# One SBUF tile of 128 bytes for five small code tiles, and the norm weights allocated ahead of the output weights

## The chip, the core and the metric

The program runs on one core of one Trainium2 chip. The metric is device time in microseconds, the median over several executions. The kernel before has a median of 848.24 us over 3 runs (843.49 to 848.28).

## The reference, cut to what matters

Four layers work on `x` of shape (2, 256, 512) with a context of (2, 512, 512), each on a normalised `x` and with a residual. Layer 0 is an attention with quantised inputs followed by a linear layer whose 4-bit weights come from a look-up table. Layer 1 is a latent attention of 16 heads and a gated feed-forward layer of inner width 1376 with ternary weights. Layer 2 is the large one, an attention of 32 query heads of 128 in 8 groups of key and value heads:

```python
q = rmsnorm(x @ q_proj.T) * q_norm_w      # 32 heads of 128
k = rmsnorm(ctx @ k_proj.T) * k_norm_w    # 8 heads of 128
v = ctx @ v_proj.T                        # 8 heads of 128
x = x + softmax(q @ k.T * 128 ** -0.5 + mask) @ v @ o_proj.T
```

It is followed by a routing step that selects tokens, a small convolutional gate, and a linear layer with eight low-rank experts (the tail).

## The kernel before, in words

The kernel is written engine by engine. Each layer is a function with one block; in a block every engine has its own list of instructions, and semaphores join them. All loads go through the queue of SyncE. The order on each engine is written out by hand, and nothing in it depends on the address of a tile.

**Tiles and their addresses.** `Core.sbuf` (line 87) takes a tile from a stack: the tile begins where the one before it ended, rounded up to a multiple of 32 bytes within the partition. A tile that lives as long as the kernel is taken from the outer stack, one of a layer from the layer's own, which is given back at its end. So every tile behind a changed one moves with it. `Codes.__init__` (line 111) takes five tiles of 128 x 4 float32, 16 bytes in each partition, that is 5 x 32 = 160 bytes of addresses. They hold scales of the feed-forward layer of layer 1 (lines 122 to 160, 1435 and 1464). Behind them come the small tiles of the ternary weights and then all tiles of all layers. Only `context_parts` (line 941) is taken from the other end of the memory and has an address of its own.

**Layer 2.** `layer2_attention` (line 1650) runs 16 steps, one per group of heads and batch. TensorE makes every float32 product from two rounded parts of each operand, in three matmuls of type float32r: `product` (line 1867, the matmul is line 1873). In each matmul 128 columns of a stationary tile are loaded as weights, and a moving tile of 256 or 512 columns is streamed past them. The products and their tiles, moving tile first, are: keys and values from `wkv2` and `context_parts` (256 columns, 48 matmuls a step), queries from `wq2` and `xnT2` (512 columns), scores from `keysT2` and `queriesT2` (512), the mix of values from `probsT2` and `values2` (256 columns, 48 matmuls a step), and the output from `wo2` and `headsT` (512). Between them stand transposes of 128 x 128 (lines 1929 and 1950). ScalarE, VectorE and GpSimd empty the banks and make the parts; VectorE also counts for the selection of tokens that the tail needs (line 2487). `norm_weights` (line 1677) is a tile of 8 bytes, loaded by two small transfers at the start of layer 2 (line 1746) and read by the scaling of the keys.

**Other places.** The tail makes its last products in the same way, from `wb` and `xnT_parts` (line 2720) and from `bm_parts` and `lowT` (line 2744). Layer 1 makes its latent queries from `latentT` and `wqk` (line 1076).

Of the kernel before, what the change touches and what calls it, by code (L numbers as in the profile page):

```python
# [13 lines left out]
F32, BF16, I32, U16, F32R = mybir.dt.float32, mybir.dt.bfloat16, mybir.dt.int32, mybir.dt.uint16, mybir.dt.float32r  # L14
# [4 lines left out]
P = 128  # L19
B, SEQ, D = 2, 256, 512  # L20
CTX = 512
TILES = B * SEQ // P
# [10 lines left out]
class Own:  # L33


    def __init__(self, engine, semaphore):
        self.engine, self.semaphore, self.count = engine, semaphore, 0
# [71 lines left out]
class Codes:  # L109

    def __init__(self, k):
        small = lambda name: k.sbuf("codes_" + name, [P, TILES], F32)
        self.beta, self.betae, self.binv, self.gate_scale, self.up_scale = (
            small(x) for x in ("beta", "betae", "binv", "gate_scale", "up_scale"))
        self.beta_ready, self.codes_ready, self.turned_psum, self.turned_ready, self.gate_psum, self.up_psum, \
            self.scales_ready = (k.keep("codes_" + x) for x in (
                "beta_ready", "codes_ready", "turned_psum", "turned_ready", "gate_psum", "up_psum", "scales_ready"))
# [1521 lines left out]
def layer2_attention(k, dram):  # L1639
# [17 lines left out]
    with ExitStack() as s:  # L1657
        ctxT2, wq, wkv = gw.ctxT2, gw.wq, gw.wkv
        xnT2 = k.sbuf("xnT2", [P, 2, KT, TILES * P], F32R, s)
        wo = k.sbuf("wo2", [P, 2, REP, D], F32R, s)  # L1660
        raw_o = gw.raw_q
        rows = k.xn
# [11 lines left out]
        keysT = k.sbuf("keysT2", [P, 2, B * CTX], F32R, s)  # L1674
        values = k.sbuf("values2", [P, 2, CTILES, HD], F32R, s)
        mask = k.sbuf("mask", [P, TPB, CTX], F32, s)
        weights = k.sbuf("norm_weights", [P, 2], F32, s)
        keyscale = weights
        probs = k.sbuf("probs2", [P, 3, CTX], F32, s)
        probsT = k.sbuf("probsT2", [P, 2, 2, CPB, SEQ], F32R, s)  # L1680
# [1294 lines left out]
def build(nc, dram, out):  # L2975
    ternary = nc.dram_tensor("ternary", (INNER, D), BF16, kind="Internal").ap()
    inverse = nc.dram_tensor("inverse_sums", (P, 8), F32, kind="Internal").ap()
    with ExitStack() as stack:
        k = Core(nc, stack)
        k.inverse_dram = inverse  # L2980

        def run(*layers):
            for layer in layers:
                k.begin(layer)
                layer(k, dram)

        with ExitStack() as context:
            with ExitStack() as first:
                k.ternary = TernaryWeights(k, first, dram, ternary)
                k.latent = LatentWeights(k, first)  # L2990
                run(layer0)
                k.context = ContextParts(k, context)
                run(layer1_attention)
            with ExitStack() as third:
                k.group_weights = GroupWeights(k, third, dram)
                run(layer1_ffn, layer2_attention)
        k.out = out
        run(tail)
# [62 lines left out]
```

How the kernel before makes its waits and increments, by code:

```python
    def wait(self):  # L43
        self.engine.wait_ge(self.semaphore, self.count)
# [79 lines left out]
def codes_magnitude_scalar(k, n, t, absolute):  # L124
    k.nc.scalar.wait_ge(k.tile_xn, TILES * n + t + 1)
    if t:
        k.nc.scalar.wait_ge(k.codes.beta_ready, t)
    k.nc.scalar.activation(absolute, k.xn[:, t, :], ACT.Abs, accum_out=k.codes.beta[:, t:t + 1])\
     .then_inc(k.codes.beta_ready, 1)
# [2 lines left out]
def codes_inverse_vector(k, h):  # L132
    v, own, q, half = k.nc.vector, k.vown, k.codes, half_of(h)
    v.wait_ge(q.beta_ready, TPB * (h + 1))
    own(v.tensor_scalar(q.beta[:, half], q.beta[:, half], 1.0 / D, None, ALU.mult))
    own.wait()
    own(v.tensor_scalar(q.betae[:, half], q.beta[:, half], EPS, None, ALU.add))
    own.wait()
    own(v.reciprocal(q.binv[:, half], q.betae[:, half]))
    own.wait()
# [29 lines left out]
def codes_turn_tensor(k, t, codes, bank):  # L170
    pe = k.nc.tensor
    pe.wait_ge(k.codes.codes_ready, t + 1)
    for f in range(KT):
        last = pe.transpose(bank.bitcast(BF16)[:, f * P:(f + 1) * P], codes[:, f * P:(f + 1) * P], k.ident16[:, :])
    last.then_inc(k.codes.turned_psum, 1)
# [2 lines left out]
def codes_turned_scalar(k, t, bank):  # L178
    a = k.nc.scalar
    a.wait_ge(k.codes.turned_psum, t + 1)
    a.copy(k.gate_up.turned[t], bank.bitcast(BF16).rearrange("p (f c) -> p f c", f=KT)).then_inc(k.codes.turned_ready, 1)
# [42 lines left out]
    def wait(self):  # L224
        value = self.base + self.count
        self.engine.wait_ge(self.semaphore, value if self.i is None else self.i * self.per + value)
```

## Time and profile before

| what | value |
|---|---|
| median of 3 runs | 848.24 us (843.49 to 848.28) |
| the profiled execution: its time, and its span | 848.75 us, 846.6 us |
| mean granted TensorE clock, as a share of full speed | 0.979 |
| TensorE matmul busy | 776.7 us |
| VectorE busy | 692.8 us |
| ScalarE busy | 517.6 us |
| GpSimd busy | 431.9 us |
| bytes moved by DMA | 60.51 MB, 71 GB/s over the span |

Layer 0 lasts to about 65 us, the attention of layer 1 to 190, its feed-forward layer to about 231, layer 2 to 772, and the tail to the end. The time of an execution is 2.15 us longer than its span. Matmuls are pipelined and their ends are modelled, so a matmul's own duration is longer than its distance to the next one. Where a row of the timeline joins x matmuls, its length is (x - 1) distances and one duration; the distance from one start to the next is called the pitch below.

### The profile page before, as it was taken

The numbers are of one execution on the slowest core, as the hardware profiler recorded it, in microseconds if no ns is written. First come the engines' busy times: TensorE is split into PE (matmuls) and PEld (weight loads), VectorE is DVE, ScalarE is ACT, GpSimd is POOL, SyncE is SP. The second block draws the span as 40 slices with busy tenths as digits, with TensorE's granted clock in tenths as the row PEclk, the third lists the DMA queues.
The fourth block names the chain that finished last, engine by engine and source line by source line (L and its number), as shares of the span: only waits on it lengthen the run. The fifth ranks groups of instructions, "written<-read, shape, count | busy, mean of one in ns | idle before, by whom it ended". The sixth has DMA issues, their size and how long they took to land. (4 is left out here: it accounts for less than half of the span.)

```text
span 846.6 us, 16363 instructions
## 1 busy us (share of the span) xinstructions
PE 776.7 (92%) x5140; PEld 633.9 (75%) x5140; DVE 692.8 (82%) x1767; ACT 517.6 (61%) x1399; POOL 431.9 (51%) x388
## 2 busy tenths in 40 slices
PE   1987799978988999999999999999999999978888
PEld 0485566644677898898888989989889889866347
DVE  7878898989987887887887887788878878876986
ACT  6865789856466657657657657665675675641421
POOL 3136058924236745754745746745754764665110
PEclk9998999989999999999999999999999999999999
DMA  8245145403111220320320320320310210003001
GB/s 312 98 128 185 49 137 173 136 23 120 32 70 25 77 76 3 97 75 0 99 75 0 99 75 0 99 71 4 99 50 25 75 50 25 26 1 111 11 0 50
DMA packets 33452, 60.51 MB, mean 71 GB/s; under 512 B 5313, under 2 KB 14593, under 8 KB 33282
## 3 DMA queue, kind: packets, MB, share of 16 engines
q1 hardware_dynamic: 33410, 59.99, 21.7%
q8 instruction: 21, 0.34, 0.2%
q14 instruction: 21, 0.17, 0.1%
HBM read 57.47 MB, written 2.52 MB: 71 GB/s over the span
## 5 line engine op out<-in xcount | busy, mean ns | idle before, releaser
L2487 DVE TENSOR_SCALAR_CACHE_REDUCE xn<-ctxT,candidate 128x512 bf16<-128x512 f32 x240 | 168.8, 741 | 0.0
L2134 ACT ACTIVATE layer_attention_probs<-xnT,stats 128x512 f32<-128x512 f32 x128 | 94.1, 735 | 113.1 <-DVE stats L2269 113.1
L2281 DVE TENSOR_TENSOR layer_attention_probsT<-bank,layer_attention_probsT 128x512 fp32r<-128x512 f32 x128 | 88.1, 688 | 52.8 <-ACT layer_attention_probsT L2142 51.5
L1873 PE MATMUL bank<-layer_attention_keysT,layer_attention_queriesT 128*128 128x512 f32 x384 | 120.0, 420 | 4.6 <-DVE layer_attention_queriesT L2262 4.6
L1873 PEld LDWEIGHTS bank<-layer_attention_probsT,layer_attention_values 128*128 128x128 f32 x768 | 98.8, 189 | 13.0 <-DVE layer_attention_probsT L2281 3.7
L2142 ACT CAST layer_attention_probsT<-bank 128x512 fp32r<-128x512 f32 x128 | 75.0, 586 | 54.7 <-PE bank L1950 54.5
L1873 PE MATMUL bank<-layer_attention_probsT,layer_attention_values 128*128 128x256 f32 x768 | 102.3, 282 | 4.0 <-DVE layer_attention_xnT L2327 2.1
L1873 PE MATMUL bank<-layer_attention_l_wq,layer_attention_xnT 128*128 128x512 f32 x408 | 99.3, 392 | 0.0
L1873 PE MATMUL bank<-layer_attention_l_wkv,layer_context_parts 128*128 128x256 f32 x720 | 93.5, 282 | 0.0
L1873 PEld LDWEIGHTS bank<-layer_attention_l_wkv,layer_context_parts 128*128 128x128 f32 x720 | 91.1, 188 | 2.5
L1873 PE MATMUL bank<-layer_attention_wo,layer_attention_headsT 128*128 128x512 f32 x336 | 88.7, 405 | 0.0
L2269 DVE CUSTOM_DVE_ANT_0 xnT<-bank,layer_attention_mask 128x512 f32<-128x512 f32 x128 | 87.1, 680 | 0.6 <-PE bank L1873 0.5
L1873 PEld LDWEIGHTS bank<-layer_attention_l_wq,layer_attention_xnT 128*128 128x128 f32 x408 | 75.3, 188 | 15.8 <-issue 0.2
L1816 POOL TENSOR_TENSOR layer_attention_mixed<-layer_attention_mixed,xnT 128x512 f32<-128x512 f32 x30 | 48.8, 1626 | 71.3 <-DMA xnT<-inverse_sums 43.8
L1950 PE MATMUL bank<-ident,layer_attention_probs 128*128 128x128 f32 x512 | 77.3, 274 | 3.1 <-ACT layer_attention_probs L2134 3.1
L1950 PEld LDWEIGHTS bank<-ident,layer_attention_probs 128*128 128x128 f32 x512 | 62.2, 141 | 14.2 <-issue 4.1
L1873 PEld LDWEIGHTS bank<-layer_attention_keysT,layer_attention_queriesT 128*128 128x128 f32 x384 | 62.6, 190 | 10.9 <-issue 5.5
L1873 PEld LDWEIGHTS bank<-layer_attention_wo,layer_attention_headsT 128*128 128x128 f32 x336 | 59.9, 188 | 11.5
L1801 POOL TENSOR_SCALAR layer_attention_ssq<-layer_attention_ssq 128x4 f32<-128x4 f32 x48 | 9.8, 205 | 89.0 <-ACT layer_attention_squares L2093 89.0
L2093 ACT ACTIVATE layer_attention_squares<-bank 128x128 f32<-128x128 f32 x192 | 52.0, 297 | 0.0
L1316 ACT ACTIVATE layer_attention_probs<-bank,layer_attention_negmax 128x512 f32<-128x512 f32 x64 | 44.8, 705 | 11.8 <-DVE layer_attention_negmax L1202 11.5
L1803 POOL TENSOR_TENSOR layer_attention_ssq<-layer_attention_ssq,minus_half 128x4 f32<-128x4 f32 x48 | 48.8, 1017 | 4.0
(352 smaller groups left out, 1648.5 us busy)
## 6 DMA issues: line engine op xcount, KB each, us to landing
layer_attention_l_raw_qo<-in_wqT SPq DMA_DIRECT2D x8, 1024.0 KB, 5.5
layer_attention_l_raw_qo<-in_woT SPq DMA_DIRECT2D x8, 1024.0 KB, 6.5
xnT<-inverse_sums SPq DMA_DIRECT2D x15, 512.0 KB, 3.7
tw_raw<-in_w_gateT SPq DMA_DIRECT2D x8, 688.0 KB, 4.0
tw_raw<-in_w_upT SPq DMA_DIRECT2D x8, 688.0 KB, 4.0
tw_raw<-in_w_downT SPq DMA_DIRECT2D x6, 768.0 KB, 5.0
layer_attention_l_raw_kv<-in_wkvT SPq DMA_DIRECT2D x8, 512.0 KB, 5.2
layer_ctx<-in_ctx SPq DMA_DIRECT2D x2, 1024.0 KB, 8.9
```

What stands on the lines that cost most here:

```text
L1316: a.activation(probs[:, u % 4, :], S[u % 3][:, :], ACT.Exp, bias=negmax[:, tile(u), head(u):head(u) + 1], accum_out=sums[:, tile(u), head( ...
L1801: own(g.tensor_scalar(ssq[:, c, :], ssq[:, c, :], 1.0 / HD, EPS, ALU.mult, ALU.add))
L1803: own(g.tensor_tensor(ssq[:, c, :], ssq[:, c, :], k.minus_half[:, 0:REP], ALU.pow))
L1816: g.tensor_tensor(now, now, factors, ALU.mult).then_inc(S_["mix_scaled"], 1)
L1873: last = pe.matmul(out, stationary[f][a], moving[f][b], start=f == 0 and x == 0, stop=f == count - 1 and x == 2)
L1950: last = pe.transpose(T[u % 2][:, c * P:(c + 1) * P], probs[:, u % 3, c * P:(c + 1) * P], k.ident[:, :])
L2093: return a.activation(squares[:, h, :], source, ACT.Square, accum_out=ssq[:, c, h:h + 1])
L2134: a.activation(probs[:, u % 3, :], masked[:, u % 2, :], ACT.Exp, bias=negmax[:, u:u + 1], scale=-1.0, accum_out=sums[:, u:u + 1]).then_inc ...
L2142: a.copy(probsT[:, 0, p % 2, :, u % 2 * P:(u % 2 + 1) * P], T[u % 2][:, :].rearrange("p (c q) -> p c q", c=CPB)).then_inc(S_["probsT_high" ...
L2269: v.tensor_tensor_reduce(masked[:, u % 2, :], S[u % 2][:, :], mask[:, u % TPB, :], -1.0, 3.4e38, ALU.add, ALU.min, negmax[:, u:u + 1]).the ...
L2281: v.tensor_tensor(probsT[:, 1, p % 2, :, columns], T[u % 2][:, :].rearrange("p (c q) -> p c q", c=CPB), probsT[:, 0, p % 2, :, columns], A ...
L2487: own(k.nc.vector.tensor_scalar((k.flags if flags is None else flags)[:, r % 2], row_tile(k.ctxT, r), k.candidate[:, r:r + 1].bitcast(F32) ...
```

## The change: what it does

The five code tiles become the first five rows of one tile of 128 x 8 x 4 float32, which takes 128 bytes. `norm_weights` is taken right behind `xnT2` instead of behind `mask`. No instruction is added, removed or moved on any queue.

```diff
 class Codes:
     def __init__(self, k):
-        small = lambda name: k.sbuf("codes_" + name, [P, TILES], F32)
-        self.beta, self.betae, self.binv, self.gate_scale, self.up_scale = (
-            small(x) for x in ("beta", "betae", "binv", "gate_scale", "up_scale"))
+        small = k.sbuf("codes", [P, 8, TILES], F32)
+        self.beta, self.betae, self.binv, self.gate_scale, self.up_scale = (small[:, x, :] for x in range(5))
...
         xnT2 = k.sbuf("xnT2", [P, 2, KT, TILES * P], F32R, s)
+        weights = k.sbuf("norm_weights", [P, 2], F32, s)
         wo = k.sbuf("wo2", [P, 2, REP, D], F32R, s)
...
         mask = k.sbuf("mask", [P, TPB, CTX], F32, s)
-        weights = k.sbuf("norm_weights", [P, 2], F32, s)
         keyscale = weights
```

All tiles behind the code tiles begin 32 bytes lower, since 128 bytes stand where 160 stood. In layer 2 the 32 bytes of `norm_weights` make up for it from `wo2` to `mask`, which keep their addresses; behind `mask` the tiles are again 32 bytes lower. The first byte of the tiles that matter, within the partition, and its remainder by 64:

| tile | before | after |
|---|---|---|
| `context_parts` (stationary for keys and values) | 196576 (32) | the same |
| `wkv2` (moving for keys and values) | 76096 (0) | 76064 (32) |
| `xnT2`, `wq2` | 96576 (0), 59712 (0) | 96544 (32), 59680 (32) |
| `raw_kv`, `raw_qo` (landing places of weights) | 84288 (0), 88384 (0) | 84256 (32), 88352 (32) |
| `wo2`, `headsT` | 112960 (0), 139648 (0) | the same |
| `keysT2`, `queriesT2` | 151936 (0), 131456 (0) | the same |
| `values2` (stationary for the mix) | 160128 (0) | the same |
| `probs2`, `probsT2` (moving for the mix) | 172448 (32), 178592 (32) | 172416 (0), 178560 (0) |
| layer 0: `bits`, `tree`, `weightT` | 149536, 166048, 215200 (32) | 32 lower (0) |
| layer 1 attention: `latentT`, `wqk`, all others | 131392, 90432 (0) | 32 lower (32) |
| tail: `raw_wb`, `wb`, `xnT_parts`, `lowT`, `bm_parts` | 105632, 113824, 136480, 157856, 161952 (32) | 32 lower (0) |

## Rows read from the trace of the kernel before

**Rows 1.** The page, busy time of each engine.
```profile
PE 776.7 (92%) x5140; PEld 633.9 (75%) x5140; DVE 692.8 (82%) x1767; ACT 517.6 (61%) x1399; POOL 431.9 (51%) x388
```

**Rows 2.** Windows by stage; columns as in the first line.
```profile
core 0: us, PE busy (x) PEld busy (x) DVE busy (x) ACT busy (x) POOL busy (x), PEclk, DMA share, GB/s
0.00:65.00 65.00, 43.24 (x243) 29.65 (x244) 51.05 (x101) 46.22 (x71) 18.14 (x26) 0.95 0.52 182
...
300.00:730.00 430.00, 429.35 (x2762) 382.84 (x2760) 348.56 (x967) 271.45 (x818) 250.40 (x219) 1.00 0.17 53
...
772.00:846.00 74.00, 64.05 (x330) 41.24 (x328) 56.32 (x178) 22.06 (x60) 9.48 (x15) 0.95 0.16 49
```

**Rows 3.** Waits of TensorE, 231 to 772 us: total, times, longest; the longest row.
```profile
PE bank L1873 <- DVE layer_attention_queriesT L2262: 4.6, 4, 2.0
```

**Rows 4.** Instruction groups, shapes apart: float32r products, count, busy us, mean ns.
```profile
L1873 PE MATMUL bank<-layer_attention_probsT,layer_attention_values 128*128 128x256 f32 x768 | 102.3, 282 | 4.0 <-DVE layer_attention_xnT L2327 2.1 <-DVE layer_attention_probsT L2281 1.2
...
L1873 PE MATMUL bank<-layer_attention_l_wq,layer_attention_xnT 128*128 128x512 f32 x408 | 99.3, 392 | 0.0
...
L1873 PE MATMUL bank<-layer_attention_l_wkv,layer_context_parts 128*128 128x256 f32 x720 | 93.5, 282 | 0.0
...
L1634 PE MATMUL bank<-layer_attention_l_wkv,layer_context_parts 128*128 128x256 f32 x48 | 6.8, 291 | 0.0
```

**Rows 5.** Timeline of TensorE in layer 2: start us, length us, what, xcount.
```profile
451.24 2.70 PE L1873 MATMUL bank<-layer_attention_l_wq,layer_attention_xnT 128*128 128x512 f32 x11
...
454.00 0.60 PE L1950 MATMUL bank<-ident,layer_attention_probs 128*128 128x128 f32 x4
...
466.41 1.45 PE L1873 MATMUL bank<-layer_attention_probsT,layer_attention_values 128*128 128x256 f32 x11
...
468.96 2.26 PE L1873 MATMUL bank<-layer_attention_wo,layer_attention_headsT 128*128 128x512 f32 x9
...
476.55 2.92 PE L1873 MATMUL bank<-layer_attention_l_wkv,layer_context_parts 128*128 128x256 f32 x23
```

**Rows 6.** Timeline of TensorE in layer 1 and in the tail, same columns.
```profile
81.51 0.64 PE L1076 MATMUL bank<-layer_attention_latentT,l_wqk 128*128 128x256 f32 x4
...
208.81 2.97 PE L190 MATMUL bank<-layer_attention_gate_up,layer_ffn_x4T 128*128 128x512 bf16 x13
...
832.06 5.30 PE L2720 MATMUL bank<-tail_wb,tail_xnT_parts 128*128 128x512 f32 x22
...
840.42 2.47 PE L2744 MATMUL bank<-tail_bm_parts,tail_lowT 128*128 128x512 f32 x10
```

**Rows 7.** Instruction groups, shapes apart: other engines at either address class.
```profile
L2281 DVE TENSOR_TENSOR layer_attention_probsT<-bank,layer_attention_probsT 128x512 fp32r<-128x512 f32 x128 | 88.1, 688 | 52.8 <-ACT layer_attention_probsT L2142 51.5
...
L2142 ACT CAST layer_attention_probsT<-bank 128x512 fp32r<-128x512 f32 x128 | 75.0, 586 | 54.7 <-PE bank L1950 54.5
...
L2262 DVE TENSOR_TENSOR layer_attention_queriesT<-bank,layer_attention_queriesT 128x512 fp32r<-128x512 f32 x32 | 22.1, 692 | 27.1 <-ACT layer_attention_queriesT L2126 27.1
...
L2126 ACT CAST layer_attention_queriesT<-bank 128x512 fp32r<-128x512 f32 x32 | 19.2, 599 | 19.2 <-PE bank L1929 18.7
...
L1772 POOL TENSOR_TENSOR layer_attention_l_wkv<-layer_attention_l_raw_kv,layer_attention_l_wkv 128x1024 fp32r<-128x1024 f32 x7 | 16.9, 2410 | 5.3 <-ACT layer_attention_l_wkv L2152 5.3
...
L667 DVE COPY_PREDICATED layer_tree<-layer_bits,layer_tree 128x2048 f32<-128x2048 uint16 x4 | 9.9, 2484 | 0.0
...
L950 POOL TENSOR_TENSOR layer_context_parts<-ctxT,layer_context_parts 128x1024 fp32r<-128x1024 f32 x4 | 9.5, 2372 | 0.3
...
L667 DVE COPY_PREDICATED layer_tree<-layer_bits,layer_tree 128x1024 f32<-128x1024 uint16 x4 | 5.3, 1313 | 0.1
```

**Rows 8.** Weight loads: their issues (KB, us to landing) and a reader's idle time.
```profile
layer_attention_l_raw_qo<-in_woT SPq DMA_DIRECT2D x8, 1024.0 KB, 6.5
...
tail_raw_wb<-in_wbT SPq DMA_DIRECT2D x1, 1024.0 KB, 7.5
...
L2164 ACT CAST layer_attention_wo<-layer_attention_l_raw_qo 128x2048 fp32r<-128x2048 f32 x7 | 13.4, 1914 | 0.0
```

## The prediction, made before the changed kernel ran

> **What bounds the kernel now.** I began with the page's busy times: TensorE is busy for 776.7 us, 92% of the span [rows 1]. That is an average over stages, so I cut the span into windows by stage [rows 2]. The reader is to see two things there. From 300 to 730 us TensorE is busy for 429.35 of 430 us at a full clock of 1.00 (2.4 GHz), while VectorE has 348.56 us of work. In layer 0 and in the tail no engine is full. So layer 2 lasts as long as the matmuls take to pass through TensorE. The waits of TensorE agree: from 231 to 772 us its longest entry is 4.6 us, in four waits [rows 3]. Whatever changes the rate of the matmuls in layer 2 reaches the end of the kernel in full, and what changes another engine there by a few per cent does not.
>
> Then I read the timeline of TensorE for the pitch of each product, since the mean duration of a matmul says nothing on its rate: both products of 256 columns show 282 ns [rows 4]. A row of x matmuls gives (length - one duration) / (x - 1). With 0.39 us for a matmul of 512 columns and 0.28 us for one of 256:
> - queries (2.70 - 0.39) / 10 = 231 ns, output (2.26 - 0.39) / 8 = 234 ns, mix (1.45 - 0.28) / 10 = 117 ns, keys and values (2.92 - 0.28) / 22 = 120 ns [rows 5];
> - tail, `wb`: (5.30 - 0.39) / 21 = 234 ns; tail, `bm_parts`: (2.47 - 0.39) / 9 = 231 ns; layer 1, `latentT`: (0.64 - 0.28) / 3 = 120 ns; a bf16 product of 512 columns, with its duration of 0.38: (2.97 - 0.38) / 12 = 216 ns [rows 6].
>
> So a float32r matmul of 512 columns needs 15 to 18 ns more than one in bf16, and the amount is not the same for each pair of tiles. The pairs `wb` and `xnT_parts` in the tail and `wq2` and `xnT2` in layer 2 have the same shapes and the same three-part loop, and differ by 3 ns. What differs is the distance of their addresses: 36864 bytes (9 x 4096) for the 231 ns of the queries, 4096 for the 231 ns of `bm_parts`, and 26688 and 22656, no multiples of 4096, for the two at 234 ns. This is why I don't cost the change at nothing from the start: it moves tiles against each other.
>
> **The change part by part.** *Instructions, queues, waits.* None is added, removed or moved. The three transfers at the start of layer 2 (mask and two norm weights) keep their places on SyncE's queue, and GpSimd's list is the same. Cost 0, and this needs no cover.
>
> *The one code tile.* Its readers are scalar operands of the feed-forward layer and get another address. Cost 0.
>
> *Pairs whose distance stays.* `wq2` and `xnT2` move together; `wo2`, `headsT`, `keysT2`, `queriesT2` stay; `latentT` and `wqk`, `wb` and `xnT_parts`, `bm_parts` and `lowT` move together. What could change is their remainder by 64. The rows exclude a price for that: `wq2` and `xnT2` both begin at a multiple of 64 and `bm_parts` and `lowT` both 32 beyond one, and both pairs have 231 ns; `wo2` with `headsT` and `wb` with `xnT_parts` are such a couple at 234 ns [rows 5, 6]. Cost 0.
>
> *Pairs whose distance changes.* There are two. The mix goes from 18464 to 18432 bytes (`probsT2` to `values2`), and keys and values from 120480 to 120512 (`context_parts` to `wkv2`). The mix has 768 matmuls, keys and values 720 + 48 = 768 [rows 4]. No row has their new distances. The pitches seen at 256 columns are 117 and 120 ns [rows 5, 6], so within what was seen the mix can lose 3 ns and keys and values can win 3 ns: 768 x 3 = 2.3 us, up for the one and down for the other. The outer bounds are wider. Below is the pitch of transposes of 128 x 128 of the same type, (0.60 - 0.27) / 3 = about 109 ns [rows 5]: (117 - 109) x 768 + (120 - 109) x 768 = 6.1 + 8.4 = 14.5 us gained. Above, I let the same excess double: 14.5 us lost. I take 0 for the sum: the nearest rows are the two pairs' own pitches and that of `latentT` and `wqk`, which lie within 3 ns and don't say which way a pair goes. The ends for the range are -2.3 and +2.3 us from the nearest rows, and -14.5 and +14.5 from the far ones.
>
> The Trainium skill ("SBUF — State Buffer", section "Who interferes with whom") says that TensorE has two read ports, one for the moving operand and one for the weight load, which are independent, and that TensorE waits for no other engine. By that the distance of two tiles has no price, and this part is exactly 0; the 3 ns between two pairs of the same shapes are not explained by it, so I keep the bounds of the rows.
>
> *Writes and reads of the other engines at the other remainder.* `probsT2` begins 32 bytes beyond a multiple of 64, `queriesT2` at one: VectorE writes them in 688 and 692 ns, ScalarE in 586 and 599. GpSimd makes a part of `context_parts` (32) in 2372 ns and of `wkv2` (0) in 2410 [rows 7]. There is no gain in being at 0; the difference is 2% and the other way. In layer 2 this is hidden behind TensorE in any case; without that cover it would be 128 x 4 ns = 0.5 us on VectorE. Cost 0.
>
> *Layer 0, `tree`.* This is not covered. The choice between leaves takes (2484 - 1313) / 1024 = 1.14 ns per element at remainder 32 [rows 7], and no row has it at 0. At one element in 1.04 ns, the slope that 688 ns for 512 leaves if its fixed part is 155 ns (my estimate from that row), the groups shown would win 9% of 9.9 + 5.3 = 15.2 us, or 1.4 us. The other end is the same loss. By the rows on the remainder I take 0.
>
> *Loads.* Weights come to land at remainder 32. A load of 1 MB to remainder 0 took 6.5 us, one to remainder 32 took 7.5 us among others in the tail [rows 8]. At worst each load is 1.0 us later; ScalarE, which reads them, shows 0.0 us of idle time before those reads [rows 8], so they are early. Cost 0; if that slack were gone, what is late next is ScalarE's rounding and then GpSimd's, at 1.0 us per group.
>
> The sum is 0 against the profiled execution of 848.75 us, which lies 0.5 us above the median of 848.24. I keep the median as the base: **848 us**.
>
> **The rivals.** *Equal remainders pay (faster).* After the change the two tiles of every float32r pair have the same remainder by 64; before, the mix (32 and 0) and keys and values (0 and 32) did not. If that made the whole excess over 109 ns go, 14.5 us are won: about 834 us; half of it gives 841. For it: the two pairs are unequal now and lie 8 and 11 ns above the transposes. Against it: the pairs that are already equal still need 231 to 234 ns where bf16 needs 216, and `latentT` with `wqk`, equal too, needs 120 [rows 5, 6]. Chance of more than 1%: 0.11.
>
> *The two streams collide more (slower).* The mix comes to a distance of 9 x 2048 bytes. If the moving stream and the weight load then meet more often, the place is the 768 mixes, and with keys and values 1536 matmuls in a stage that TensorE fills. The nearest row is `latentT` with `wqk`, at 20 x 2048: 120 ns, so +2.3 us, 850.5 us. It decides from 5.5 ns on each of the 1536, 8.5 us; with the excess doubled it gives 863 us. Against it: no pair of 256 columns shows more than 120 ns. Chance of more than 1%: 0.07.
>
> *Only layers 0 and tail gain.* Then 1.4 us at most in layer 0, about 847. It lies within the forecast.
>
> *The change does nothing at all*, because no tile moves: excluded by the rounding to 32 bytes, 160 against 128, and it would give the same 848.
>
> **How the numbers follow.** Below 1%, about 8.5 us, a measurement of this kernel can't tell a difference from none; its runs span 843.49 to 848.28. The forecast (sum 0, within 2.3 us for each pair, 1.4 us in layer 0) has 0.82, all of it within 1%. The faster rival has 0.11, the slower 0.07. The range takes the run spread with the near bounds (843.5 - 2.3 - 1.4 = about 840 below) and half of the slower rival's far bound above (848.2 + 7.3 = about 855); beyond it lie the two rivals' far halves and less than 2 in 10.
>
> **What would show it.** In the timeline of layer 2 the mix should stay at 117 to 120 ns and keys and values too; queries at 231 and output at 234 must not move at all, or distance is not what matters. The window from 300 to 730 us should still show TensorE full. VectorE's 688 ns and ScalarE's 586 ns for `probsT2` should be the same within 2%, and the 2484 ns of the choice in layer 0 shows whether the remainder counts there. The prediction is wrong if the mix or keys and values come near 109 ns, or over 123.

## The result and the profile after

The changed kernel takes 849.88 us (median of 21 runs, 846.71 to 852.72), the kernel before 847.48 us over 21 runs beside it. The ratio is 1.0028, with an interval of 1.0016 to 1.0040: slower by 2.4 us, which these runs can tell from none. The time lies within 1% and inside the range. The forecast of no difference at all is refuted. The profiled execution took 849.88 us, its span is 847.7 us and its mean granted clock 0.976.

The page of the changed kernel, then its windows by stage, then the longest wait of TensorE in layer 2, against [rows 1 to 3]:

```profile
PE 777.4 (92%) x5134; PEld 634.9 (75%) x5140; DVE 692.1 (82%) x1767; ACT 516.9 (61%) x1399; POOL 432.0 (51%) x388
```
```profile
0.00:65.00 65.00, 42.73 (x247) 28.50 (x248) 53.66 (x110) 47.78 (x73) 19.29 (x28) 0.97 0.53 188
300.00:730.00 430.00, 429.30 (x2758) 382.60 (x2757) 347.84 (x966) 271.06 (x819) 250.74 (x219) 1.00 0.16 52
772.00:846.00 74.00, 65.11 (x328) 41.45 (x325) 55.75 (x177) 21.96 (x60) 9.46 (x15) 0.93 0.15 45
```
```profile
PE bank L1872 <- DVE layer_attention_queriesT L2261: 4.6, 4, 2.0
```

TensorE is as full as before. The row to read is the count: in the same 430 us it starts 2758 matmuls where [rows 2] had 2762. So each takes a little longer, and that shows in no busy time. A count depends on where the window cuts a step, though; the period of a step, below, is the better measure.

The timeline of TensorE in layer 2 of the changed kernel, against [rows 5]:

```profile
441.12 2.99 PE L1872 MATMUL bank<-layer_attention_l_wkv,layer_context_parts 128*128 128x256 f32 x24
...
452.96 2.92 PE L1872 MATMUL bank<-layer_attention_l_wq,layer_attention_xnT 128*128 128x512 f32 x12
...
464.25 1.60 PE L1872 MATMUL bank<-layer_attention_probsT,layer_attention_values 128*128 128x256 f32 x12
```

The mix now has (1.60 - 0.28) / 11 = 120 ns where it had 117. Keys and values have (2.99 - 0.28) / 23 = 118 ns where they had 120. Queries stay at (2.92 - 0.39) / 11 = 230 ns. Two pairs got another distance, and the pitches of those two moved, in opposite directions.

What the pitches come to is read from the period of a step. In each step SyncE issues one transfer of the sums of the softmax, so two such rows twelve steps apart give the mean step. The timeline of SyncE, first of the kernel before, then of the changed one:

```profile
303.07 0.34 SPq L1729 DMA_DIRECT2D inverse_sums<-stats  x1
...
699.73 0.34 SPq L1729 DMA_DIRECT2D inverse_sums<-stats  x1
```
```profile
300.71 0.34 SPq L1728 DMA_DIRECT2D inverse_sums<-stats  x1
...
697.91 0.34 SPq L1728 DMA_DIRECT2D inverse_sums<-stats  x1
```

Before: (699.73 - 303.07) / 12 = 33.055 us. After: (697.91 - 300.71) / 12 = 33.100 us. Over 16 steps that is +0.7 us. Two traces of kernels with the same distances in layer 2 agree within 0.012 us a step (the run "All layers but layer 2" below against before), so 0.045 is more than their spread. The trace splits it: I summed the distance from each matmul's start to the next one's over these twelve steps, product by product. A step's mix takes 5.791 us instead of 5.691 (16 x 0.100 = +1.6 us), keys and values 5.658 instead of 5.738 (-1.3 us), and all other matmuls together 0.025 us more (+0.4 us). So the two pairs make +0.3 of the +0.7 us.

The other engines did not change. Groups of instructions of the changed kernel, shapes apart, against [rows 7]:

```profile
L2280 DVE TENSOR_TENSOR layer_attention_probsT<-bank,layer_attention_probsT 128x512 fp32r<-128x512 f32 x128 | 88.1, 688 | 53.1 <-ACT layer_attention_probsT L2141 51.9
...
L2141 ACT CAST layer_attention_probsT<-bank 128x512 fp32r<-128x512 f32 x128 | 74.9, 585 | 55.7 <-PE bank L1949 55.7
...
L1771 POOL TENSOR_TENSOR layer_attention_l_wkv<-layer_attention_l_raw_kv,layer_attention_l_wkv 128x1024 fp32r<-128x1024 f32 x7 | 16.8, 2403 | 5.6 <-ACT layer_attention_l_wkv L2151 5.6
...
L666 DVE COPY_PREDICATED layer_tree<-layer_bits,layer_tree 128x2048 f32<-128x2048 uint16 x4 | 9.9, 2472 | 0.0
...
L666 DVE COPY_PREDICATED layer_tree<-layer_bits,layer_tree 128x1024 f32<-128x1024 uint16 x4 | 5.3, 1326 | 0.1
```

Each is within 1% of its row before, with its tile 32 bytes lower.

**The rest of the 2.4 us.** The two profiled executions differ by 1.1 us. Up to the first load of layer 2 the changed kernel is 2.4 us ahead, its steps lose 0.65 us, the end of layer 2 loses 1.2 us and the tail 1.7 us. The last two go with TensorE's granted clock, and the first at least in part (0.97 in layer 0 where [rows 2] had 0.95). Windows over the end of layer 2 and the first part of the tail, before and after:

```profile
732.56:771.80 39.24, 31.36 (x180) 25.49 (x178) 31.95 (x72) 13.53 (x33) 29.14 (x24) 1.00 0.04 14
771.80:825.03 53.23, 45.91 (x235) 26.12 (x235) 43.35 (x146) 17.65 (x52) 9.48 (x15) 0.94 0.17 49
```
```profile
730.80:771.21 40.41, 32.75 (x180) 27.10 (x178) 31.95 (x72) 13.52 (x33) 29.16 (x24) 0.96 0.05 14
758.40:761.80 3.40, 3.40 (x14) 3.01 (x13) 3.23 (x6) 0.96 (x2) 3.32 (x4) 0.50 0.00 0
771.21:826.10 54.89, 47.53 (x234) 26.59 (x235) 43.36 (x146) 17.56 (x52) 9.46 (x15) 0.91 0.16 47
```

The same 180 matmuls take 1.2 us longer, and the middle row shows why: from 758.4 to 761.8 us the clock is 0.50 (1.2 GHz). The timeline shows what TensorE did ahead of it, before and after:

```profile
758.99 1.67 PE L1873 MATMUL bank<-layer_attention_probsT,layer_attention_values 128*128 128x256 f32 x12 [2.12 <-DVE layer_attention_xnT L2327]
```
```profile
757.23 2.00 PE L1872 MATMUL bank<-layer_attention_probsT,layer_attention_values 128*128 128x256 f32 x12 [2.12 <-DVE layer_attention_xnT L2326]
```

It had waited for the same 2.12 us in both, and the clock fell in one of them. So a single profile says little outside the steps. Over the 216 runs of the whole kernel in these comparisons (each kernel with its own mean, one slope for all), 0.001 less of mean clock goes with 0.51 us more of the span (standard error 0.03). At a clock of 0.979 the kernel before stands at 845.8 us (87 runs) and the changed one at 847.25 (21 runs, standard error 0.27): +1.4 us.

### The profile page after: what moved, and what is told of

It is laid out like the page before. It is cut to its first block and busy times, and to the rows that moved or that the text cites. A ratio compares the mean times of both kernels' runs of the same rounds, so it can differ in the third digit from the quotient of the medians.

```text
span 847.7 us, 16357 instructions
## 1 busy us (share of the span) xinstructions
PE 777.4 (92%) x5134; PEld 634.9 (75%) x5140; DVE 692.1 (82%) x1767; ACT 516.9 (61%) x1399; POOL 432.0 (51%) x388
## 5 line engine op out<-in xcount | busy, mean ns | idle before, releaser
L2280 DVE TENSOR_TENSOR layer_attention_probsT<-bank,layer_attention_probsT 128x512 fp32r<-128x512 f32 x128 | 88.1, 688 | 53.1 <-ACT layer_attention_probsT L2141 51.9
L1872 PE MATMUL bank<-layer_attention_keysT,layer_attention_queriesT 128*128 128x512 f32 x384 | 120.1, 421 | 4.6 <-DVE layer_attention_queriesT L2261 4.6
L1872 PEld LDWEIGHTS bank<-layer_attention_probsT,layer_attention_values 128*128 128x128 f32 x768 | 100.6, 190 | 12.5 <-DVE layer_attention_probsT L2280 3.9
L2092 ACT ACTIVATE layer_attention_squares<-bank 128x128 f32<-128x128 f32 x192 | 51.9, 297 | 0.0
```

The costliest lines, as they stand in the source:

```text
L1872: last = pe.matmul(out, stationary[f][a], moving[f][b], start=f == 0 and x == 0, stop=f == count - 1 and x == 2)
L2092: return a.activation(squares[:, h, :], source, ACT.Square, accum_out=ssq[:, c, h:h + 1])
L2280: v.tensor_tensor(probsT[:, 1, p % 2, :, columns], T[u % 2][:, :].rearrange("p (c q) -> p c q", c=CPB), probsT[:, 0, p % 2, :, columns], A ...
```

## The experiments

Theory 1 says that the distance between the moving and the stationary tile sets the pitch of a float32r product, and that TensorE hands this on to the end. Its rivals change with the question; each expectation names them. The first three edits are shown against the changed kernel.

**Only the code tiles.** `norm_weights` goes back to its old place, so that keys and values alone get their new distance.

```diff
 xnT2 = k.sbuf("xnT2", ...)
-weights = k.sbuf("norm_weights", [P, 2], F32, s)
 wo = k.sbuf("wo2", ...)
...
 mask = k.sbuf("mask", ...)
+weights = k.sbuf("norm_weights", [P, 2], F32, s)
```

> The code tiles alone: all later tiles 32 bytes lower, norm weights left behind the mask. Keys and values get the new distance (120512), the mix keeps its old one (18464). Theory 1 (only the distance of the two tiles of a product counts): keys and values near 118 ns as in the changed kernel, the mix at 117 as before, so 768 x 2 = 1.5 us faster than before, ratio about 0.998; a step of layer 2 about 0.1 us shorter. Theory 2 (the 32 bytes cost something in the other layers, some 1.7 us): about the same as before, ratio 1.000. Theory 3 (addresses count for nothing, the change was chance): ratio 1.000 and both pitches as before.

Measured: 847.79 us, ratio 0.9998 (0.9980 to 1.0016). The time alone doesn't choose between the theories, whose ratios of 0.998 and 1.000 both lie in the interval; the pitches speak for theory 1. In the timeline keys and values have (1.58 - 0.28) / 11 = 118 ns, the mix (1.57 - 0.28) / 11 = 117 ns:

```profile
465.46 1.57 PE L1872 MATMUL bank<-layer_attention_probsT,layer_attention_values 128*128 128x256 f32 x12
...
471.25 1.58 PE L1872 MATMUL bank<-layer_attention_l_wkv,layer_context_parts 128*128 128x256 f32 x12
```

**Only the norm weights.** The five code tiles are five again, so that the mix alone gets its new distance.

```diff
-small = k.sbuf("codes", [P, 8, TILES], F32)
-self.beta, ... = (small[:, x, :] for x in range(5))
+small = lambda name: k.sbuf("codes_" + name, [P, TILES], F32)
+self.beta, ... = (small(x) for x in ("beta", ...))
```

> The norm weights alone: the code tiles as before, tiles from the output weights to the mask 32 bytes higher, all others as before. The mix gets the new distance (18432), keys and values keep the old one. Theory 1: the mix near 120 ns, keys and values at 120, so 768 x 3 = 2.3 us slower, ratio about 1.0027, a step of layer 2 about 0.14 us longer. Theory 2: the same 2.3 us, since no other layer moves. Theory 3: ratio 1.000.

Measured: 850.10 us, ratio 1.0027 (1.0009 to 1.0045). The mix has (1.60 - 0.28) / 11 = 120 ns:

```profile
465.72 1.60 PE L1873 MATMUL bank<-layer_attention_probsT,layer_attention_values 128*128 128x256 f32 x12
```

The SyncE rows of the two, codes first:

```profile
302.41 0.34 SPq L1728 DMA_DIRECT2D inverse_sums<-stats  x1
...
698.40 0.34 SPq L1728 DMA_DIRECT2D inverse_sums<-stats  x1
```
```profile
301.87 0.34 SPq L1729 DMA_DIRECT2D inverse_sums<-stats  x1
...
699.77 0.34 SPq L1729 DMA_DIRECT2D inverse_sums<-stats  x1
```

Their steps are 32.999 and 33.158 us, -0.056 and +0.103 against before. The sum, +0.047, is the changed kernel's +0.045. So the change is two changes of opposite sign, and the norm weights alone make it slower.

**All layers but layer 2.** The code tiles are merged, and layer 2 is put back by a pad of 32 bytes ahead of its first tile, with the norm weights behind `mask` again. The feed-forward layer of layer 1, whose tiles stand behind the pad, is put back with it. (`self.begin` is the address of a tile of that layer; it moves with the pad.)

```diff
-self.begin = base + 4 * KT * (2 * GW2 + ...)
+self.begin = base + 32 + 4 * KT * (2 * GW2 + ...)
...
+sb("pad", [P, 8], F32)
 self.wq = sb("wq2", [P, 2, KT, GW2], F32R)
...
 xnT2 = k.sbuf("xnT2", ...)
-weights = k.sbuf("norm_weights", [P, 2], F32, s)
...
 mask = k.sbuf("mask", ...)
+weights = k.sbuf("norm_weights", [P, 2], F32, s)
```

> Layer 0, the attention of layer 1 and the tail 32 bytes lower as in the changed kernel; a pad of 32 bytes ahead of the weights of layer 2 puts all tiles of the feed-forward layer and of layer 2 back to their old addresses. Theory 1: no product of layer 2 changes its distance, so 0, ratio 1.000. Theory 2: 1.7 us slower, ratio 1.002, found in the stages before 231 us or after 772 us. Theory 3: 1.000.

Measured: 847.41 us, ratio 1.0001 (0.9983 to 1.0018), a step of 33.067 us. Other addresses in layer 0, the attention of layer 1 and the tail cost nothing that this ratio can tell, with 1.5 us to either side. At equal clock (the table at the end) the run stands 0.7 us above before, less than two standard errors.

**The distance alone.** A kernel without the layers: TensorE runs groups of float32r products on zeros, with the strides of the mix, keys and values, queries and output, and moves only the distance. No other engine works meanwhile, and nothing of the reference is computed.

```python
...
for i, (a, b) in enumerate(((0, 0), (0, 1), (1, 0))):
    s = base + a * stationary[0] + f * stationary[1] + n % 2 * P
    m = base + MOVING + shift + b * moving[0] + f * moving[1]
    pe.matmul(to[:, 0:wide], area[:, s:s + P], area[:, m:m + wide], ...)
...
```

> Nothing of the reference is computed: a kernel of products alone, on zeros, with no other engine at work, in the shapes and strides of the mix, of keys and values, of the queries and of the output, with the distance of moving and stationary tile stepped through a multiple of 4096 plus 0 to 480 bytes by 32; for the mix also 4 to 28 bytes by 4, 512, 1024, 2048 and 2080 bytes, and 0 and 32 bytes with both tiles 32 bytes further on. Theory 1: the pitch depends on the distance: the mix near 120 ns at 0 and 117 at 32, keys and values 118 at 320 and 120 at 352, queries 231 at 0, output 234 at 448; both tiles moved together change nothing. The theory of equal remainders by 64: low at every multiple of 64, high between. The theory that the two read ports are independent: one pitch for all distances.

One execution, at a mean clock of 1.00. The distance is counted from the stationary to the moving tile. The timeline of TensorE, six groups of the mix (256 columns) at distances of 0, 32, 96, 192, 256 and 288 beyond a multiple of 4096, and between them two of the output (512 columns) at 0 and 32:

```profile
39.35 3.12 PE L3020 MATMUL bank<-area 128*128 128x256 f32 x24
...
50.55 2.98 PE L3020 MATMUL bank<-area 128*128 128x512 f32 x12
...
54.17 3.04 PE L3020 MATMUL bank<-area 128*128 128x256 f32 x24
...
65.28 3.04 PE L3020 MATMUL bank<-area 128*128 128x512 f32 x12
...
83.72 3.13 PE L3020 MATMUL bank<-area 128*128 128x256 f32 x24
...
128.38 2.99 PE L3020 MATMUL bank<-area 128*128 128x256 f32 x24
...
157.95 3.11 PE L3020 MATMUL bank<-area 128*128 128x256 f32 x24
...
172.77 3.04 PE L3020 MATMUL bank<-area 128*128 128x256 f32 x24
```

The rows at 0 and 256 agree (3.12, 3.11), and so do those at 32 and 288 (3.04 both). Mean pitch in ns from start to start, without the first matmul of a group:

| distance by 256 | 0 | 32 | 64 | 96 | 128 | 160 | 192 | 224 |
|---|---|---|---|---|---|---|---|---|
| mix | 119.8 | 116.5 | 117.8 | 120.0 | 118.5 | 118.6 | 114.3 | 118.4 |
| keys and values | 119.6 | 117.8 | 117.7 | 119.6 | 120.0 | 118.6 | 117.8 | 118.7 |
| queries | 230.7 | 233.2 | 229.7 | 233.2 | 232.1 | 233.1 | 232.7 | 232.5 |
| output | 227.7 | 233.7 | 229.8 | 233.3 | 231.7 | 233.1 | 233.4 | 232.6 |

From 256 to 480 the same values return within 0.4 ns; adding 512, 1024 or 2048 bytes to the mix's distance, or moving both tiles by 32, changes nothing beyond 0.3 ns. The change took the mix from 18464 to 18432 bytes, that is from 32 to 0 by 256, and keys and values from 96 to 64 (`wkv2` stands 120480 and then 120512 bytes below `context_parts`). The table gives +3.3 and -1.9 ns for that; the kernel shows 117 to 120 and 120 to 118. So these differences need no other engine, and they repeat every 256 bytes. It also refutes "equal remainders pay": 0, 64, 128 and 192 have equal remainders by 64 and give 119.8, 117.8, 118.5 and 114.3. The Trainium skill ("SBUF — State Buffer", section "Who interferes with whom") has the moving port and the weight load's port independent, by which every entry of a row would be the same. The measurement decides: the entries are not the same. Whether the two ports meet, or something else makes the difference, no run here shows.

**Four pairs at their best distances.** Pads alone, from the kernel before: 96 bytes ahead of `wq2`, 192 ahead of `xnT2`, 192 ahead of `squares`, 160 ahead of `probs2`.

```diff
-self.begin = base + 4 * KT * (2 * GW2 + ...)
+self.begin = base + 96 + 4 * KT * (2 * GW2 + ...)
...
+sb("pad", [P, 24], F32)
 self.wq = sb("wq2", [P, 2, KT, GW2], F32R)
...
+k.sbuf("pad_x", [P, 48], F32, s)
 xnT2 = k.sbuf("xnT2", ...)
 wo = k.sbuf("wo2", ...)
...
+k.sbuf("pad_o", [P, 48], F32, s)
 squares = k.sbuf("squares", ...)
...
+k.sbuf("pad_p", [P, 40], F32, s)
 probs = k.sbuf("probs2", ...)
```

> The kernel before with pads alone, so that four pairs of layer 2 stand at the best distances of the sweep: by remainder of the distance by 256, mix 32 to 192, keys and values 96 to 192, output 192 to 0, queries 0 to 64. Theory 1 (the pitch of a pair goes by its distance with a period of 256 bytes and TensorE's time passes to the end): mix 116.75 to 114.3 ns (768 x 2.45 = 1.9 us), keys and values 120.0 to 118.7 (1.0 us), output 233.4 to 227.7 (384 x 5.7 = 2.2 us), queries 230.7 to 229.7 (0.4 us): 5.5 us less, about 842 us, ratio 0.9935. Theory 2 (the pitches of the lone sweep are lost in the kernel to other waits of TensorE, or the time is set by other things that move with the addresses): the pitches may change, the time stays within 1 us, ratio 0.999 to 1.001.

Measured: 846.04 us, ratio 0.9992 (0.9968 to 1.0015), a step of 32.900 us: -0.155 where theory 1 had -0.34. By product, in us a step against before: mix -0.095 (expected -0.12), keys and values -0.152 (-0.06; the table's own 119.6 and 117.8 ns give -0.09), output -0.075 (-0.14), queries +0.044 (-0.03), and the scores, whose distance did not change, +0.099. The sweep gave the signs of three of four, not the sizes. The ratio itself lies where theory 2 had it. At equal clock (below) the time is 2.9 us less, near the 2.5 us of the steps, and that speaks against theory 2; what failed of theory 1 is the step worked out from the sweep.

**Layer 2's distances alone, the change again, and the mix put back.** The first is the kernel before with the norm weights moved and 224 bytes ahead of `wq2`, the second the changed kernel unaltered, the third the changed kernel with one line more. First and third:

```diff
-self.begin = base + 4 * KT * (2 * GW2 + ...)
+self.begin = base + 224 + 4 * KT * (2 * GW2 + ...)
...
+sb("pad", [P, 56], F32)
 self.wq = sb("wq2", [P, 2, KT, GW2], F32R)
...
 xnT2 = k.sbuf("xnT2", ...)
+weights = k.sbuf("norm_weights", [P, 2], F32, s)
...
 mask = k.sbuf("mask", ...)
-weights = k.sbuf("norm_weights", [P, 2], F32, s)
```
```diff
 mask = k.sbuf("mask", ...)
+k.sbuf("pad_p", [P, 8], F32, s)
 probs = k.sbuf("probs2", ...)
```

> Complement of the run in which only the other layers were moved: all other layers keep the addresses of before, layer 2 has the distances of the changed kernel (its tiles stand 224 bytes higher instead of 32 lower, the same by 256). Theory 1: pitches as in the changed kernel (mix 119.8, keys and values 117.9), and if the pitches are all, +0.7 us, ratio 1.0008. Theory 3 (layer 2's new addresses cost something beside the two pitches): +1.9 to +2.4 us, ratio 1.0022 to 1.0028.

> The changed kernel once more, unaltered, beside the others. If the part of its 1.0028 that the pitches don't explain (about 1.2 to 1.7 us) is chance of the half-clock stretches, theory 1 expects about 1.0008 here; if it belongs to the program, 1.0028 again.

> The changed kernel with a pad of 32 bytes between the mask and the probabilities, so that the mix has its old distance again (remainder 32) while norm_weights stays in its new place. Theory 1: mix back to 116.75 ns, keys and values 117.9, the slower time is gone: about -0.9 us against before, ratio 0.999. Theory 3 (the new place of norm_weights or the shift costs by itself): the mix returns, but the time stays 1 us or more above before, ratio 1.001 to 1.002.

Measured, in this order: 851.03 us and 1.0044 (1.0025 to 1.0063), 850.60 us and 1.0031 (1.0006 to 1.0055), 846.62 us and 1.0002 (0.9977 to 1.0027). The steps are 33.103, 33.109 and 33.024 us. So the slower time comes back whenever layer 2 has the new distances, also when it stands 224 bytes higher instead of 32 lower, and it goes when the mix alone gets its old distance. The last interval alone would not show that; all runs together do: the four kernels with the mix at 0 (changed, again, layer 2 alone, norm weights alone) lie above 1 with their whole intervals, and none of the others does. Theory 1's +0.7 us is missed by all repeats, which lie at 1.0028 to 1.0044. A part of that is clock: their mean granted clocks are 0.9780 (first measurement), 0.9775 (again) and 0.9756 (layer 2 alone), against 0.9789 to 0.9807 for the kernel before. At a clock of 0.979 they stand 1.4, 1.1 and 0.8 us above it, with standard errors of 0.3 to 0.4.

**The scores put back, and the mix at its best.** The first is the run of four pairs with the queries at their old distance, and with 224 bytes ahead of `wo2`, which puts `keysT2` and `queriesT2` at their old place by 256. The second is the changed kernel with 192 bytes ahead of `probs2`. The first against the run of four pairs, the second against the changed kernel:

```diff
-k.sbuf("pad_x", [P, 48], F32, s)
 xnT2 = k.sbuf("xnT2", ...)
+k.sbuf("pad_x", [P, 56], F32, s)
 wo = k.sbuf("wo2", ...)
```
```diff
+k.sbuf("pad_p", [P, 48], F32, s)
 probs = k.sbuf("probs2", ...)
```

> As the run with four pairs at the best distances (a step of layer 2 of 32.900 us where before has 33.055), with two things put back: the distance of wq2 and xnT2 is 0 again, and keysT2 and queriesT2, whose distance had not changed, stand 512 bytes higher than before instead of 480, the same place by 256. In that run the scores took 6.439 us a step where before took 6.340, and the queries 5.558 where before took 5.514. Theory A (the place of the two tiles by 256 counts too, not their distance alone, and distance 0 is better for the queries): scores 6.34 and queries 5.51 again, the step at 32.76 us, 0.30 less than before, 16 x 0.30 = 4.8 us, about 842.3 us, ratio 0.9944. Theory B (the scores were slower because faster products made TensorE wait for others there): scores stay near 6.44, the step at 32.86, 3.2 us, ratio 0.9962.

> The changed kernel with a pad of 192 bytes between the mask and the probabilities, so that the mix stands at remainder 192 instead of 0 and all else stays as the change has it. If the pair's distance sets its time: mix 5.60 us a step where the changed kernel takes 5.79, keys and values 5.66, the step 33.10 - 0.19 = 32.91 us, 0.14 less than before, 2.3 us, ratio 0.997. If the change costs something beside the two pairs: 1 us or more above that, ratio 0.9985 or higher.

Measured: 844.22 us, ratio 0.9959 (0.9936 to 0.9981) for the first, which beats both kernels; 848.79 us, ratio 1.0000 (0.9975 to 1.0025), at a mean clock of 0.9758, for the second. By the ratio alone the second would be the rival's case (0.9985 or higher); at equal clock it stands 1.7 us below before, as its step has it. Their timelines of SyncE, in this order:

```profile
299.92 0.34 SPq L1733 DMA_DIRECT2D inverse_sums<-stats  x1
...
693.80 0.34 SPq L1733 DMA_DIRECT2D inverse_sums<-stats  x1
```
```profile
300.72 0.34 SPq L1729 DMA_DIRECT2D inverse_sums<-stats  x1
...
696.26 0.34 SPq L1729 DMA_DIRECT2D inverse_sums<-stats  x1
```

Steps of 32.823 and 32.962 us, 3.7 and 1.5 us less than before over 16. The first lies between theory A (32.76) and theory B (32.86): the queries came back to 5.522 us, as A says, the scores only to 6.413, near B's 6.44. Two products that the edit left at their distance changed as well: the output lost 0.049 us a step, and keys and values won 0.066 (5.586 to 5.520) at the very same addresses. The timeline of TensorE in the first run shows how keys and values can:

```profile
442.94 1.58 PE L1877 MATMUL bank<-layer_attention_l_wkv,layer_context_parts 128*128 128x256 f32 x12
...
467.79 1.54 PE L1877 MATMUL bank<-layer_attention_l_wkv,layer_context_parts 128*128 128x256 f32 x12
...
472.17 2.89 PE L1877 MATMUL bank<-layer_attention_l_wkv,layer_context_parts 128*128 128x256 f32 x24
```

These groups have (1.58 - 0.28) / 11 = 118, 115 and 113 ns at one distance by 256. In the run of four pairs it is the group of 24 that has 118 and the groups of 12 that have 114. So at 192 a group has one of two pitches, the sweep showed one of them, and what chooses between them is open. At 64, as in the changed kernel, every group has 118.

In the second the mix takes the expected 5.603 us a step and keys and values 5.661, but the step wins 0.137 of the expected 0.19 against the changed kernel. A part of what the products win is given back. The waits of TensorE, 231 to 772 us (total, times, longest), in the changed kernel, in the one with the mix at 192 and in the one with four pairs and the scores put back:

```profile
PE bank L1872 <- DVE layer_attention_probsT L2280: 1.1, 2, 0.9
```
```profile
PE bank L1873 <- DVE layer_attention_probsT L2281: 2.2, 8, 1.0
```
```profile
PE bank L1877 <- DVE layer_attention_probsT L2285: 3.8, 9, 1.2
```

TensorE comes to the mix before VectorE has made its operand: 8 and 9 waits instead of 2. The distance from the last matmul of a scores group to what follows grows with it, from 250 ns in the changed kernel to 253 and 257. So the next limit of the step is the chain that makes this operand. VectorE is its last link, but it waits for ScalarE there (51.9 of 53.1 us of its idle time, above); which link to shorten was not tested. The same gap holds most of what the scores lost in the run of four pairs: 248.9 ns before and 258.4 there, eight times a step, is 0.076 of the 0.099 us.

The mean step against the time, all layer kernels. The fourth column is the difference of the mean spans at a clock of 0.979, by the slope above, standard error about 0.4:

| kernel | step, us | 16 x difference to before | span at equal clock | ratio |
|---|---|---|---|---|
| changed | 33.100 | +0.7 | +1.4 | 1.0028 |
| changed again | 33.109 | +0.9 | +1.1 | 1.0031 |
| layer 2's distances alone | 33.103 | +0.8 | +0.8 | 1.0044 |
| norm weights alone | 33.158 | +1.7 | +1.2 | 1.0027 |
| other layers alone | 33.067 | +0.2 | +0.7 | 1.0001 |
| mix put back | 33.024 | -0.5 | -0.3 | 1.0002 |
| code tiles alone | 32.999 | -0.9 | -0.5 | 0.9998 |
| mix at 192 | 32.962 | -1.5 | -1.7 | 1.0000 |
| four pairs | 32.900 | -2.5 | -2.9 | 0.9992 |
| four pairs, scores put back | 32.823 | -3.7 | -3.1 | 0.9959 |

At equal clock the time follows the step within 0.7 us in every line; the ratios alone do not, since the mean clocks differ (0.9756 to 0.9802).

## Why the prediction was wrong

*What bounds the kernel:* right for this change. What the products lose and win is the change of the step, and at equal clock +-0.1 us per step is seen at the end. With faster products it holds in part: the mix at 192 won 0.19 us a step and the step 0.137.

*No instruction, queue or other engine changes its cost:* right. The 688 and 586 ns are 688 and 585, and the choice in layer 0 takes 2472 and 1326 ns where it took 2484 and 1313; the rival "only layers 0 and tail gain" has nothing to stand on. Moving the other layers alone gives 1.0001.

*Pairs whose distance stays:* right. Queries and output take 0.3% more in the changed kernel's steps.

*Pairs whose distance changes:* **this step failed**, in the words "I take 0 for the sum". The bounds were right: the mix lost 1.6 us of the 2.3 allowed, keys and values won 1.3 of the 2.3. The runs showed +0.3 us for the two pairs and +0.7 for the steps in the place of the 0; the 0.4 between them lies in the step's other matmuls, which I had at 0 as well. The 0 was taken since I held that the nearest rows "don't say which way a pair goes". For the mix they did say it: `latentT` with `wqk` stands at 20 x 2048 bytes with 120 ns [rows 6], the mix went to 9 x 2048, and it got 120 ns. That was in the slower rival, with the price of +2.3 us, and I gave it weight only from 1% on. That a row of a product with other strides carries over is known from the sweep alone, and not as a rule: at 0 the mix is nearly at its worst and the output at its best. For keys and values no row had the new distance by 256; the sweep was needed.

*Equal remainders pay:* refuted by the sweep. *The two streams collide more:* the mix did what this rival says (117 to 120 ns), but keys and values, which it takes with it, went the other way, and 5.5 ns was not reached. Its 850.5 us lies near the measured 849.88 by luck: it is the mix alone, without what keys and values won and without the clock.

*The numbers:* 848.0 us against 849.88, and 0.82 on "within 1%", which 1.0028 is. What failed is the sign and size of a difference below that 1%. The signs of being wrong that I named, 109 and 123 ns, were not met: they were too wide to see 3 ns on 768 matmuls.

*What stays open:* in the measured 2.4 us the step explains 0.7. At equal clock the three measurements of layer 2's new distances give 1.2 us on average (standard error about 0.25), so some 0.4 us may be left over in the rest. It may lie in the other layers: moved alone they stand at +0.7 where the step gives +0.2 (standard error 0.4), and layer 2's distances without them leave nothing over. The remainder of the 2.4 us goes with the lower mean clock of the runs. Whether the change lowers it isn't settled: the four kernels with the mix at 0 have 0.9756 to 0.9780, four of the others 0.9791 to 0.9802, but the mix at 192 has 0.9758 and the four pairs 0.9773. Open too is what makes a group of keys and values take 114 or 118 ns at the same addresses, so that the sweep's 117.8 ns at 192 is 116.4 and 115.0 ns on average in the two runs.

## What to carry to other kernels

Where TensorE bounds a stage, a moved tile is a changed instruction: list for each product the distance of its two tiles by 256, before and after, and look for a row at the new distance, of a product with the same strides if there is one, before taking 0. A single pad can be worth more than a removed matmul (0.12 us): the mix at remainder 192 instead of 0 saves 0.14 us a step. Measure what is won at the end, not on the product, as a wait elsewhere takes a share back, and compare runs of like clock where the difference is below half a per cent.

## What the runs showed of the hardware

- With no other engine at work, the pitch of a float32r matmul with its weight load went from 114 to 123 ns at 256 columns and from 228 to 234 ns at 512, when only the distance of the two tiles was moved (one execution). Steps of 4 bytes count too: the mix has 122.9, 120.1, 117.3, 118.8, 121.8, 120.1 and 117.0 ns at 4 to 28 bytes.
- The pattern repeats every 256 bytes within 0.4 ns and depends on the strides of the product: at 0 the output has its best pitch (227.7 ns) and the mix nearly its worst (119.8 ns).
- Distance is not all: at 192, groups of keys and values ran at 113 to 115 ns and at 118 ns in the same execution, and which group had which differed between two kernels with both tiles at the same addresses.
- That the place of both tiles counts beside their distance isn't shown. Keys and queries, moved together by 480 bytes, went from 6.340 to 6.439 us a step, but most of that is waiting for the operand of the mix, and 6.413 stayed when they were put back to their place by 256. In the sweep, both tiles moved by 32 changed 0.3 ns at most.
